# A GNN and mixture-of-experts kernel on one core: the loop over 48 columns of the adjacency build, unrolled by the program before, run by the engines' own loop after

## The reference, cut to what matters

```
x, src, dst                      # 6250 nodes x 256, 100000 edges, sorted by dst
h0 = layernorm(x) @ W_in + b_in
for l in range(4):               # GNN layers
    msg  = segment_sum((h * dinv)[src], dst) * dinv
    ctx  = mean(h) @ Wg[l] + bg[l]
    z    = relu((h + msg) @ Wl[l] + bl[l] + ctx)
    h    = layernorm(z) * gamma[l] + beta[l]
x = x + h
x = x + ffn(layernorm(x))        # routing to 2 of 8 experts, 256 -> 512 -> 256, layernorm
```

## Time and profile before

| | |
|---|---|
| median of 3 runs | 3270.61 us |
| profiled execution | 3270.61 us, span 3269.0 us |
| busy, share of the span | PE 96%, DVE 61%, ACT 26%, POOL 2% |
| build, busy in 50 us (150 to 200 us) | PE 44.43 us, DVE 50.00 us, ACT 38.11 us |
| mean granted clock of PE | 0.981 |

### The profile page before, as it was taken

The page is one execution under the profiler, slowest core; times in us unless marked ns, Lnnn a source line. Parts: engine busy times, 40 slices in busy tenths (PEclk is TensorE's granted clock), DMA queues, the critical chain, the costliest instruction groups (busy, mean ns, idle before and its releaser), DMA issues.

```text
span 3269.0 us, 53555 instructions
## 1 busy us (share of the span) xinstructions
PE 3123.1 (96%) x17421; PEld 1814.9 (56%) x17421; DVE 1981.6 (61%) x5303; ACT 849.1 (26%) x1934; POOL 70.7 (2%) x168
## 2 busy tenths in 40 slices
PE   6888888799999999999999999999999999979998
PEld 4666666344444444444444444444444444468887
DVE  7999999655555455555555455555556666645554
ACT  3777777311111111111111111111111111123322
POOL 0000000000000000000000000000000000000010
PEclk8999999799999999999999999999999999989999
DMA  4222222322222222222221222222222222110000
GB/s 136 80 80 80 80 80 60 108 69 69 70 75 72 69 69 69 69 69 69 70 76 64 75 69 69 69 69 69 75 80 85 86 80 80 58 38 18 18 18 17
DMA packets 134108, 225.07 MB, mean 69 GB/s; under 512 B 12277, under 2 KB 106596, under 8 KB 134018
## 3 DMA queue, kind: packets, MB, share of 16 engines
q1 hardware_dynamic: 131666, 217.53, 20.5%
q0 software_dynamic: 2352, 6.40, 0.8%
HBM read 178.17 MB, written 45.74 MB: 68 GB/s over the span
## 4 chain that ended last, share of the span: by engine, by line
PE 92%; DVE 4%; issue 1%; ACT 1%; DMA 1%; SPq 1%; DVEq 0%; ACTq 0%; POOLq 0%; POOL 0%
PE bank L1361 63%; PE bank L1231 8%; PE bank L1435 5%; PE bank L1441 5%; PE bank L1319 4%; PE bank L1249 2%; PE bank L1217 2%; PE bank L1309 1%; DVE region L701 1%; DVE region L670 1%; PE bank L1247 1%; DMA tab<-in_x 1%; PE bank L1255 1%; ACT tab L1120 0%; PE bank L1242 0%
## 5 line engine op out<-in xcount | busy, mean ns | idle before, releaser
L1361 PE MATMUL bank<-tab,region 128*128 128x512 f16 x9604 | 2145.3, 379 | 9.7 <-DMA region<-adjacency 9.3
L1361 PEld LDWEIGHTS bank<-tab,region 128*128 128x128 fp8e4 x9604 | 940.6, 98 | 1063.3 <-DVE tab L790 18.3
L1231 PE MATMUL bank<-region 128*128 128x320 bf16 x1862 | 316.4, 319 | 57.0 <-DVE region L670 55.7
L670 DVE TENSOR_SCALAR region<-iota_w,src_col,src_w 128x640 bf16<-128x640 int16 x931 | 363.5, 447 | 0.5 <-issue 0.4
L1043 ACT ACTIVATE tab<-region 128x640 fp8e4<-128x640 uint8 x490 | 307.3, 712 | 24.1 <-DVE region L701 24.1
L891 DVE SCALAR_TENSOR_TENSOR region<-bank,c_back,bias 128x256 f32<-128x256 f32 x196 | 94.8, 484 | 351.2 <-PE bank L1319 351.2
L1231 PEld LDWEIGHTS bank<-region 128*128 128x128 f16 x1862 | 231.6, 144 | 132.9 <-DVE region L670 104.5
L1147 ACT ACTIVATE sd<-mv,eps_c 128x1 f32<-128x1 f32 x196 | 57.7, 294 | 812.2 <-DVE mv L898 812.2
L886 DVE TENSOR_TENSOR region<-bank,region 128x256 f16<-128x256 f32 x196 | 83.3, 425 | 284.8 <-ACT region L1143 284.8
L1143 ACT ACTIVATE region<-bank 128x256 f16<-128x256 f32 x196 | 75.3, 384 | 567.4 <-PE bank L1309 567.4
L1435 PE MATMUL bank<-tab 128*128 128x384 f32 (+1 forms) x544 | 178.3, 487 | 3.1 <-DMA b_s<-in_L_ffn_b 3.1
(11 more groups left out here) (193 smaller groups left out, 2140.3 us busy)
## 6 DMA issues: line engine op xcount, KB each, us to landing
region<-adjacency SPq DMA_DIRECT2D x196, 784.0 KB, 4.3
adjacency<-tab SPq DMA_DIRECT2D x12, 3136.0 KB, 13.9
region<-in_x POOLq DMA_DIRECT2D x48, 128.0 KB, 2.3
out<-region SPq DMA_DIRECT2D x48, 128.0 KB, 1.7
tab<-in_x SPq DMA_DIRECT2D x1, 6016.0 KB
tab<-in_L_ffn_W SPq DMA_DIRECT2D x4, 512.0 KB, 4.5
Wg_s<-in_L_gnn_Wg SPq DMA_DIRECT2D x1, 1024.0 KB
region<-in_L_gnn_Wl SPq DMA_DIRECT2D x1, 1024.0 KB, 5.6
```

The costliest lines, as they stand in the source:

```text
L670: ins = v.tensor_scalar(hot_s[:, j, :], iota_w[:], src_col[:, ds(start + j, 1)], src_w[:, ds(start + j, 1)], ALU.is_equal, ALU.mult)
L1231: ins = mm(bank[k % 2 * 2 + half][:, 0:HALF], hot_d[:, :, j], hot_s[:, j, half * HALF:(half + 1) * HALF], start=j == 0, stop=j == WIN - 1)
L1361: ins = mm(acc[a][:, :], A_s[:, a, m, :], tab[:, here + m, :], start=m == 0, stop=m == T - 1)
```

## The change

`columns_all` becomes `columns`, which takes the engine, and its outer loop of six passes is run by the engine: `with eng.Fori(0, MLOOP) as i`. The eight columns of a pass are still written out, so a pass is one block of code that is run six times. Column 0 stays ahead of the loop. The step functions are untouched; but i is now a register, so m = 8 * i + k is one too, and all that is worked out from it.

```diff
-        def columns_all(step):
+        def columns(eng, step):
 
             step(0, 0, 0)
-            for i in range(MLOOP):
+            with eng.Fori(0, MLOOP) as i:
                 for k in range(1, 2 * MG + 1):
                     step(i * (2 * MG) + k, k, i)
@@
-            columns_all(hots)
+            columns(dve, hots)
@@
-            columns_all(extract)
+            columns(act, extract)
@@
-            columns_all(counts)
+            columns(pe, counts)
```

## The result

| | before | after |
|---|---|---|
| median (range; runs) | 3269.91 us (3267.2 to 3272.12; 4) | 3293.8 us (3292.97 to 3294.89; 4) |
| ratio, 95% interval | | 1.0074 [1.0056, 1.0091] |
| profiled execution, its span | 3270.61, 3269.0 us | 3299.24, 3297.5 us |

The kernel is slower by 23.9 us, 0.74%. The execution that was profiled lies 5.4 us above the median of its kernel, so the trace shows some 28.5 us of difference where the timed runs show 24.

What follows compares the result with a forecast made beforehand. DVE was taken to set the pace of the build. Slow loads of 3.4 us and five missed ways back of 13.8 us sum to 17.2 us on 3270.6 us, giving 3288 us, range 3273 to 3301.

Steps and rivals of the forecast that it cites:

- A: The forecast itself: in the build, DVE's ways back miss and slow loads cost; 3288 us, between 3278 and 3299; chance 0.61.
- DVE bounds the build and has no gap for added work: In the build DVE is busy 50.00 of 50 us, so any wait for its sequencer is paid in full.
- Ordinary columns cost nothing: Between lines 693 and 658 added register instructions take 0.71 us of 1.05 us of cover, leaving 0.34: no cost.
- Slow loads, 12 x 0.28 = 3.4 us: In 12 of 48 columns the load of `starts` is slow by 0.62 us against 0.34 left: 3.4 us.
- DVE's ways back miss, 5 x 2.75: Between passes DVE must fetch code five times, 2.9 us less 0.15 of cover each: 13.8 us.
- The sign of it: On DVE at line 412, five of six branches were to take 2 to 3.5 us if its ways back miss.
- rival B: DVE's pass stays at hand, only slow loads cost: 3274 us, between 3271 and 3278; chance 0.20.
- PE's way back: 3.4 us, hidden: If PE's way back misses, its 3.4 us stop hides beside DVE's, or costs 10 us at worst if DVE alone hits.
- Rival C, PE's clock: PE's clock falls after the pause at each way back, 5 x 4 = 20 us more, 3308 us; chance 0.07.
- D: DVE's sequencer falls behind by 0.2 to 0.3 us in each of 48 columns, with misses 3300 us; chance 0.08.
- E: Faster: PE's branch at line 1300 may hit, but is covered; at most 0.4 us back, 3270 us; chance 0.04.
- Wrong if the build ends over 30 us later: The prediction's own test of failure: the build ending within 3 us of where it did, or over 30 us later.

Runs made afterwards that it cites:

- dve4: Against the kernel before, only DVE's loop run by the engine, four columns a pass, PE and ACT written out: 3272.63 us, ratio 1.0010.
- dve8: Against the kernel before, only DVE's loop run by the engine, eight columns a pass, PE and ACT written out: 3291.91 us, ratio 1.0069.
- pe8: Against the kernel before, only PE's loop run by the engine, eight columns a pass, DVE and ACT written out: 3291.08 us, ratio 1.0067.
- pe8pad64: pe8 with 64 already fulfilled waits added ahead of PE's build, which only shift its pass in the stream: 3322.15 us, one run.
- pe8pad128: pe8 with 128 already fulfilled waits added ahead of PE's build, which only shift its pass in the stream: 3288.41 us, one run.

## Why the prediction was right, and where it was not

The time predicted was 3288 us, measured 3293.8: in the range of 3273 to 3301 and in A's own, and slower. Point by point:

- **DVE bounds the build and has no gap for added work.** Right: the 44 columns are 30.8 us longer, DVE stands still in them for 27.5 us more, and the span is 28.5 us longer.
- **Ordinary columns cost nothing.** Right within what can be read: 10.89 to 10.98 us each in dve4, against 10.88 to 10.93 in most columns before.
- **Slow loads, 12 x 0.28 = 3.4 us.** Right in size where no way back is missed: 0.3 us for each of 11 in dve4, 3.3 us, and 3.4 timed. It is not all a gap: 0.1 us of it is idle, 0.1 lost overlap, and 0.1 comes behind the column's first instruction. In the kernel after only six of the eleven fall outside a way back, 1.8 us.
- **DVE's ways back miss, 5 x 2.75.** Right in kind and size: 15.3 us for 13.8. The price estimated, 2.9 us, is the 2.80 to 2.87 us from the branch to the next instruction. dve8 isolates it, dve4 takes it away.
- **The sign of it.** Wrong: line 412 should have had five branches of 2 to 3.5 us on DVE, and all six last under 0.1. Read alone, this would have spoken for rival B. Line 658, idle for "issue" five times at 3.1 us, is what decided it.
- **PE's way back: 3.4 us, hidden.** This is the step that failed. It took 7.1 to 7.4 us (the price of a forward branch, 3.4 us, was carried over to a backward one), and PE's spare time in a column does not hide 6.7: in pe8 DVE waits 4.1 us each time. With both misses it adds 1.7 us a pass at line 664 and 0.7 at 701, 12.0 us in the trace, where the sum had nothing. What the prediction set at 10 us at worst, if DVE alone hits, is 21.9 in pe8.
- **Rival C, PE's clock.** It was given 0.07 and a price of 4 us a way back. The clock does fall behind every way back, although the pause was thought too short for it, and costs 1.2 to 1.6 us each in dve8. So it is no case of its own but a part of A: small, real, and in the kernel after mixed with PE's own miss.
- **Rivals B, D, E.** B is out: 650 instructions are not kept, 488 neither. D is out: line 670 has no gaps in the passes. E: line 1300 still missed (3.06 us), covered as before; in pe8pad64 and pe8pad128 the same branch, at line 1309, took 0.45 us, so where the code lies does matter to it.
- **"Wrong if the build ends over 30 us later."** It ended at 611.3 us instead of 581.3 in the profiled execution, which stands just at that bound; that execution is 5.4 us above the median of its kernel.

The sum that should have been made: 5 x (3.05 + 1.7 + 0.7) + 6 x 0.3 = 29.1 us for the profiled execution, whose 44 columns are 30.8 us longer; most of the rest is the overlap lost at each wait. How the 23.9 us of the timed runs divide can't be read, since only the slowest execution was profiled. The prediction's 17.2 us fell short by the term that it left out, and the result stayed within its range partly by luck: the upper bound had room from other terms (3.5 us for a way back, 7.4 for the loads), not for this one.

## What to carry to other kernels

A loop run by the engine is nearly free when its body fits in what the sequencer keeps (here 326 instructions on DVE, for 3.4 us of register instructions behind slow loads, and 248 on ACT, for nothing). When it does not fit (488 on DVE, 491 on ACT, 1,720 on PE in 17 of 20 ways back), each way back stops the engine for 3.0 to 8.2 us, and the kernel paid 4.4 to 6.1 us for it (10.9 in the one run of pe8pad64). So the body is to be counted in instructions, matmuls twice, before the time saved is. When two engines miss at the same moment their prices overlap, so taking one away alone may give next to nothing: here 23.9 us for both, 22.7 and 21.9 for one. And on DVE and ACT the record of a branch isn't where to look for a miss; look at the engine's first instruction behind it.

## What the runs showed of the hardware that was not expected

- A missed branch has a short record on DVE (0.07 us, the time lying behind it) and on ACT (0.05, then 5.2 us), and a long one on PE (6.7 to 8.2 us).
- PE's miss takes 6.6 to 8.2 us going back and 3.0 to 3.9 forward.
- PE's pass of 1,720 instructions hit in some rounds and missed in others of one execution (0.22 and 8.2 us in pe8pad128), and a shift of the code by 64 instructions alone came with 31 us more (3322.15 against 3291.08, the former one run).
- A pause of PE of 2.2 us, as the timeline of dve8 has it ahead of line 1238 at 136.47 us, came before 10.2 us at half the clock, and 24 products put into the pause kept it at full in four of five cases. Pauses of 1.4 us in the kernel before came before 3.4 us at half.
- A gap of 0.1 us on DVE stands for 0.3 us of lost time, since the overlap of 0.07 to 0.1 us with the instruction before is lost too, and the next instruction is late as well.
